# Output projection and second layer norm: two passes over halves of the token tiles become one pass over single tiles

## The chip, the cores and the metric

The kernel runs on the 8 cores of one Trainium2 chip. Each core computes one of the 8 sequences of the batch, with the same program and the same weights, and the cores exchange nothing. The time is the device time of the slowest core in microseconds (us).

## What is computed

One transformer layer with the norm behind each part, on x of shape (8, 2048, 2048): attention with its own norm ahead of it, 16 heads, a band of 256 tokens and 16 global tokens; then a gated feed-forward part whose weights are integers with a scale.

```python
xn = layernorm(x) * ln_scale + ln_bias
Q, K, V = proj(Wq), proj(Wk), proj(Wv)            # of [global tokens, xn]
attn = softmax(Q K^T * scale + band_mask)
a = (attn @ V)[:, 16:] @ Wo.T + x                 # the output projection
x = layernorm(x + a)                              # = layernorm(2 x + out @ Wo.T)
x = layernorm(x + ffn(x))                         # silu(gate) * up, then down
```

The change lies in the fourth and fifth of these lines: the output projection by Wo, the sum with 2x, and the norm of that sum.

## The kernel before

The kernel is written by hand: each engine has its own stream of instructions, in the order in which the program text emits them, and counts on semaphores are all that ties the streams together. `wt(engine, token)` makes an engine wait until a semaphore has reached a count. A wait holds up everything behind it in that engine's stream. SyncE (SP) issues most of the transfers, so a wait in its stream holds up every transfer that is written behind it. `barrier()` makes all engines wait for everything before it.

The stages follow one another: the first norm and its transposes; per head the projections and the attention (its result goes to `ao_dram` in HBM, line 641); a barrier (line 649); the stage that the change touches (lines 672 to 771); a barrier (line 773); then the feed-forward part in two passes over half of the tokens each. It first reads the normed tiles back from `r2_dram` (GpSimd, line 808), transposes them on TensorE (line 1124), and then runs gate, up and down.

The stage of the change, before it: the 2048 tokens are 16 tiles of 128 rows. Wo, in bf16, is held in SBUF as four slices of 512 output columns (`woT`), loaded by 16 transfers on GpSimd's queue that cast from f32 (line 677). Two halves `th` of 8 token tiles follow each other. Within a half:

- For each half of the output columns `eh` and each of the 8 tiles `ti`, SP loads the attention result of that tile, 512 KB in bf16, into one of two buffers `aot` (line 697). TensorE makes two accumulation groups of 16 matmuls of 128x512 (line 713), one per slice of Wo, into two PSUM banks in turn, and VectorE copies each bank into the tile's slot of `v1h` (line 726). `v1h` holds 8 tiles in f32. So every attention tile is loaded twice, and the half has 32 groups.
- After that, a loop over the 8 tiles does the norm. SP loads the tile of x (1 MB, line 739, two buffers `xres`); VectorE adds 2x (line 749), takes the statistics (lines 296 and 299), ScalarE the root (line 306), VectorE the reciprocal (line 313) and the normed tile (line 760); SP stores the tile to `r2_dram` (line 767), which waits for line 760.

In SP's stream the order of this second loop is therefore: x load of tile ti, store of tile ti (behind a wait for its norm), x load of tile ti+1, its store, and so on. Behind the last store of the first half come the attention loads of the second half. The wait of the load itself (line 738) asks only for the norm two tiles back.

VectorE's first copy of the second half also waits for all stores of the first half (`t_spill_half`, line 724), because it overwrites the slots of `v1h`.

Of the kernel before, what the change touches and what calls it, by code (L numbers as in the profile page):

```python
# [10 lines left out]
ALU = mybir.AluOpType  # L11
bfdt = ml_dtypes.bfloat16

D = 2048
T = 2048
NH = 16
# [6 lines left out]
ND = D // 128  # L23
# [26 lines left out]
def wt(eng, token):  # L50
    if token is None:
        return
    sem, n = token
    if n > 0:
        eng.wait_ge(sem.h, n)
# [10 lines left out]
def build_nc(debug=False):  # L66
    nc = bass.Bass("TRN2", target_bir_lowering=False)

    x_in = nc.dram_tensor("x", [T, D], F32, kind="ExternalInput").ap()
# [21 lines left out]
    r2_dram = nc.dram_tensor("r2sp", [T, D], F32, kind=scratch_kind).ap()  # L91
    ao_dram = nc.dram_tensor("aosp", [NT, NH, 128, 128], BF16, kind=scratch_kind).ap()
# [5 lines left out]
    s_pe = Sem(nc, "s_pe")  # L98
    s_dve = Sem(nc, "s_dve")
# [10 lines left out]
    s_aot = [Sem(nc, "s_aot0"), Sem(nc, "s_aot1")]  # L110
    s_xr = [Sem(nc, "s_xr0"), Sem(nc, "s_xr1")]
    s_r2s = Sem(nc, "s_r2s")
# [33 lines left out]
    agm = sba(outer, "agt", [128, 2], F32)  # L146
    rstd = sba(outer, "rstdt", [128, 1], F32)
# [18 lines left out]
    with nc.Block() as blk:  # L166
# [34 lines left out]
        def f(sync):  # L201
            for dst, src in [(ident, id_in), (masks, mk_in), (ones_col, oc_in),
                             (ones_row, or_in), (neg128, n128_in), (lnw, lnw_in),
                             (lnb, lnb_in), (sgt, sg_in), (sut, su_in),
                             (sd_row, sd_in)]:
                s_c0.inc(sync.dma_start(out=dst[:, :], in_=src[:, :]), 16)
# [82 lines left out]
        def emit_ln_stats(get_v, tok_ready):  # L289
            def f(dve):  # L290
                wt(dve, tok_ready)
                wt(dve, ln_act_tok["prev"])
                dve.wait_ge(s_dve.h, s_dve.n)
                vv = get_v()
                for i in range(4):
                    ins = dve.bn_stats(stats[:, i * 6:(i + 1) * 6], vv[:, i * 512:(i + 1) * 512])  # L296
                s_dve.inc(ins)
                dve.wait_ge(s_dve.h, s_dve.n)
                s_dve.inc(dve.bn_aggr(agm[:, :], stats[:, :]))
            blk.vector(f)  # L300
            t_ag = s_dve.tok

            def f(act, t_ag=t_ag, t_prev=ln_dve_tok["prev"]):
                wt(act, t_ag)
                wt(act, t_prev)
                return act.activation(sqv[:, :], agm[:, 1:2], AF.Sqrt, bias=epsv[:, 0:1])
            t_sq = da_emit(f)
            ln_act_tok["prev"] = t_sq

            def f(dve):  # L310
                wt(dve, t_sq)
                dve.wait_ge(s_dve.h, s_dve.n)
                s_dve.inc(dve.reciprocal(rstd[:, :], sqv[:, :]))
            blk.vector(f)
            ln_dve_tok["prev"] = s_dve.tok
            return s_dve.tok

        xt_tok = {}
        for tt in range(NT):
            buf = tt % 2  # L320
# [10 lines left out]
            t_rstd = emit_ln_stats(lambda buf=buf: xtile[:, buf * D:(buf + 1) * D], xt_tok[tt])  # L331
# [12 lines left out]
            for c in range(ND):  # L344
                bank = trb[(tt * ND + c) % 6]
# [83 lines left out]
        for hg in range(4):  # L429
# [7 lines left out]
            for h in range(4 * hg, 4 * hg + 4):  # L437
# [9 lines left out]
                for step in range(9):  # L447
                    bank = next_sc()
# [46 lines left out]
                if h % 4 == 0:  # L495
                    for kt in range(NT + 1):
                        bank = next_sc()
# [38 lines left out]
                for q4 in range(4):  # L536
                    klist = kts(q4) + ["glob"]
                    nk = len(klist)
                    for i, kt in enumerate(klist):
                        bank = next_sc()  # L540
# [115 lines left out]
        v1h = sba(p3s, "v1ht", [128, 8 * D], F32)  # L656
        woT = sba(p3s, "woTt", [128, 2 * ND * 1024], BF16)
# [22 lines left out]
        blk.gpsimd(f)  # L680
        t_wosl = [s_wos[sl].tok for sl in range(4)]

        for th in range(2):
            for eh in range(2):

                for ti in range(8):
                    tt = th * 8 + ti
                    abuf = ti % 2

                    def f(sync, th=th, eh=eh, ti=ti, tt=tt, abuf=abuf):  # L690
                        prev = t_womm.get((th, eh, ti - 2)) or t_womm.get((th, eh - 1, 6 + ti)) \
                            or t_womm.get((th - 1, 1, 6 + ti))
                        wt(sync, prev)
                        src_ = ao_dram[tt].rearrange("h p k -> p h k")
                        dstv = aot[:, abuf * D:(abuf + 1) * D].rearrange(
                            "p (h k) -> p h k", h=NH)
                        s_aot[abuf].inc(sync.dma_start(out=dstv, in_=src_), 16)
                    blk.sync(f)
                    t_aotld[(th, eh, ti)] = s_aot[abuf].tok

                    for e2 in range(2):
                        e4 = 2 * eh + e2
                        bank = b_wo[e2]

                        def f(t, th=th, eh=eh, ti=ti, e2=e2, e4=e4, abuf=abuf, bank=bank):
                            if th == 0 and ti == 0:
                                wt(t, t_wosl[e4])
                            if e2 == 0:
                                wt(t, t_aotld[(th, eh, ti)])
                            wt(t, bank.freed)  # L710
                            off = eh * ND * 1024 + e2 * ND * 512
                            for hc in range(NH):
                                ins = t.matmul(bank.p[:, :],  # L713
                                               aot[:, abuf * D + hc * 128:abuf * D + (hc + 1) * 128],
                                               woT[:, off + hc * 512:off + (hc + 1) * 512],
                                               start=(hc == 0), stop=(hc == NH - 1))
                            bank.used = s_pe.inc(ins)
                            t_womm[(th, eh, ti)] = bank.used
                        blk.tensor(f)

                        def f(dve, th=th, eh=eh, ti=ti, e2=e2, e4=e4, bank=bank):
                            wt(dve, bank.used)
                            if eh == 0 and e2 == 0 and th >= 1:
                                wt(dve, t_spill_half.get(th - 1))
                            dve.wait_ge(s_dve.h, s_dve.n)
                            ins = dve.tensor_copy(v1h[:, ti * D + e4 * 512:ti * D + (e4 + 1) * 512],
                                                  bank.p[:, :])
                            bank.freed = s_dve.inc(ins)
                        blk.vector(f)
                        t_woev[(th, eh, ti, e2)] = s_dve.tok  # L730
                t_womm[(th, eh)] = s_pe.tok

            for ti in range(8):
                tt = th * 8 + ti
                buf = ti % 2

                def f(sync, th=th, ti=ti, tt=tt, buf=buf):
                    wt(sync, t_ln2.get((th, ti - 2)) or t_ln2.get((th - 1, 6 + ti)))
                    s_xr[buf].inc(sync.dma_start(out=xres[:, buf * D:(buf + 1) * D],
                                                 in_=x_in[tt * 128:(tt + 1) * 128, :]), 16)  # L740
                blk.sync(f)
                t_xres[(th, ti)] = s_xr[buf].tok

                def f(dve, th=th, ti=ti, buf=buf):
                    wt(dve, t_xres[(th, ti)])
                    wt(dve, t_woev[(th, 1, ti, 1)])
                    vv = v1h[:, ti * D:(ti + 1) * D]
                    dve.wait_ge(s_dve.h, s_dve.n)
                    s_dve.inc(dve.scalar_tensor_tensor(vv, xres[:, buf * D:(buf + 1) * D],
                                                       2.0, vv, ALU.mult, ALU.add))  # L750
                blk.vector(f)
                t_v1 = s_dve.tok

                t_rstd = emit_ln_stats(lambda ti=ti: v1h[:, ti * D:(ti + 1) * D], t_v1)

                def f(dve, th=th, ti=ti, t_rstd=t_rstd):
                    wt(dve, t_rstd)
                    vv = v1h[:, ti * D:(ti + 1) * D]
                    dve.wait_ge(s_dve.h, s_dve.n)
                    s_dve.inc(dve.tensor_scalar(vv, vv, agm[:, 0:1], rstd[:, 0:1],  # L760
                                                ALU.subtract, ALU.mult))
                blk.vector(f)
                t_ln2[(th, ti)] = s_dve.tok

                def f(sync, tt=tt, ti=ti, t_r2=s_dve.tok):
                    wt(sync, t_r2)
                    s_r2s.inc(sync.dma_start(out=r2_dram[tt * 128:(tt + 1) * 128, :],
                                              in_=v1h[:, ti * D:(ti + 1) * D]), 16)
                blk.sync(f)
                t_spill[(th, ti)] = s_r2s.tok  # L770
            t_spill_half[th] = s_r2s.tok

        barrier()
        p3p.close()
# [520 lines left out]
```

## Time and profile before

| | us |
|---|---|
| time before, median of 2 runs | 5431.15 |
| these 2 runs | 5306.09 and 5556.21 |
| the profiled execution, device time | 5057.47 |
| its span on the slowest core (core 2) | 5055.9 |
| spans of the 8 cores | 5029.0 to 5055.9 |
| mean granted TensorE clock of the cores | 0.909 to 0.913 |

The span runs from the first to the last instruction of a core, so 1.6 us of the profiled execution lie outside it. The profiled execution is 5% shorter than the lower one of the two timed runs, so a duration of the trace can be set against 5057.47 us only. TensorE is busy for 75% of the span, VectorE for 27%, ScalarE for 8%. The stage of the change lies between 1651 and 2176 us of the span, a tenth of it. All positions in the text are microseconds from the span's start on core 2.

### The profile page before, as it was taken

The page shows a single profiled execution, that of the slowest core. Times are in us where ns is not written, and L with a number is a line of the kernel's source. Part 1 is how long each engine was busy: PE and PEld are TensorE (multiplying, and loading weights), DVE is VectorE, ACT ScalarE, POOL GpSimd, SP SyncE. Part 2 cuts the span into 40 slices and gives each one's busy share as a digit, 9 for nine tenths or more (in the row PEclk, how much of TensorE's full clock was granted, in tenths as well). Part 3 has the DMA queues.
Part 4 walks back from the last instruction along what each step waited for, and adds up shares of the span by engine and source line. Part 5 has one row for each costly group of instructions (what it writes and reads, how often), then busy time and mean ns, then how long its engine had stood idle before and what let it go on. Part 6 is the DMA issues. An engine that isn't in the chain of part 4 may idle for free.

```text
span 5055.9 us, 44219 instructions; the slowest of 8 cores (5029.0 to 5055.9 us)
## 1 busy us (share of the span) xinstructions
PE 3768.4 (75%) x15764; PEld 1444.9 (29%) x16072; DVE 1343.3 (27%) x1936; ACT 402.7 (8%) x661; POOL 315.4 (6%) x601
## 2 busy tenths in 40 slices
PE   2288898988988536269999986556799999766640
PEld 1133232333332212123333332222233333222210
DVE  6624534444354132331111110000222221000013
ACT  0001212111122000000000000000011110000000
POOL 0000000000000000000000011111000000111110
PEclk9999898999998777669999999989999999999985
DMA  2211202102000533343333334333444443244344
GB/s 83 65 28 20 38 13 41 23 15 40 13 17 17 109 116 93 124 84 67 67 60 66 67 65 73 52 57 59 90 114 110 115 100 65 28 60 60 58 90 158
DMA packets 236584, 331.02 MB, mean 65 GB/s; under 512 B 133316, under 2 KB 178373, under 8 KB 225621
## 3 DMA queue, kind: packets, MB, share of 16 engines
q0 software_dynamic: 85856, 180.46, 22.3%
q1 hardware_dynamic: 150518, 147.72, 9.1%
q8 instruction: 136, 2.23, 0.2%
q14 instruction: 74, 0.61, 0.0%
HBM read 445.62 MB, written 58.72 MB: 100 GB/s over the span
## 4 chain that ended last, share of the span: by engine, by line
PE 65%; DMA 16%; DVE 10%; issue 6%; ACT 1%; SPq 1%; DVEq 0%; another core or an unknown queue 0%; POOL 0%; ACTq 0%; POOLq 0%
PE p_gu L913 25%; DMA wdTt<-wd 10%; PE p_wo L713 4%; PE p_sc L458 4%; PE p_sc L470 4%; PE p_sc L506 4%; PE p_gu L1023 3%; PE p_gu L916 2%; PE p_srow L1221 2%; DVE statst L296 2%; PE p_pv L1219 2%; DMA xrest<-x 2%; PE p_sc L552 2%; DVE xnfmt L362 2%; PE p_s L1023 2%
## 5 line engine op out<-in xcount | busy, mean ns | idle before, releaser
L913 PE MATMUL p_gu<-xn2ht,wgTt 128*128 128x512 bf16 x2740 | 633.1, 381 | 15.4 <-DVE rowLt L875 9.0
L913 PE MATMUL p_gu<-xn2ht,wuTt 128*128 128x512 bf16 x2766 | 635.8, 380 | 2.6
L944 DVE TENSOR_SCALAR gust<-p_gu,sutt 128x512 f32<-128x512 f32 x176 | 132.2, 751 | 1102.6 <-PE p_gu L918 1101.4
L1023 PE MATMUL p_cs<-wdTt,hmidt 128*128 128x512 bf16 x336 | 132.7, 395 | 375.5 <-DMA wdTt<-wd 300.6
L1023 PE MATMUL p_gu<-wdTt,hmidt 128*128 128x512 bf16 x1378 | 377.9, 396 | 39.9 <-DVE v2spt L1050 16.5
L913 PEld LDWEIGHTS p_gu<-xn2ht,wgTt 128*128 128x128 bf16 x2816 | 262.1, 98 | 376.5 <-issue 87.8
L913 PEld LDWEIGHTS p_gu<-xn2ht,wuTt 128*128 128x128 bf16 x2816 | 261.1, 98 | 365.6 <-issue 74.7
L713 PE MATMUL p_wo<-woTt,aott 128*128 128x512 bf16 x1004 | 230.6, 391 | 176.9 <-DMA aott<-aosp 142.9
L571 ACT ACTIVATE p_sbt<-p_sc 128x512 bf16<-128x512 f32 x352 | 203.2, 596 | 1027.6 <-PE p_sc L555 1010.2
L1050 DVE TENSOR_TENSOR v2spt<-p_cs,sd_bct 128x512 f32<-128x512 f32 x8 | 5.5, 692 | 1012.5 <-PE p_cs L1032 1012.5
L934 ACT ACTIVATE gust<-p_gu,sgtt 128x512 f32<-128x512 f32 x176 | 120.9, 687 | 1843.9 <-PE p_gu L918 1830.3
L1009 POOL DMA_DIRECT2D wdTt<-wd x352 | 185.8, 528 | 1036.3 <-PE p_x L1023 922.2
L458 PE MATMUL p_sc<-xnfmt,wqkTt 128*128 128x512 bf16 x1003 | 223.9, 381 | 27.3 <-DMA wqkTt<-wk 26.2
L1219 PE MATMUL p_pv<-p_sbt,v4t 128*128 128x512 bf16 x340 | 150.6, 443 | 105.0 <-DVE rowAt L587 83.2
L470 PE MATMUL p_sc<-xnfmt,wqkTt 128*128 128x512 bf16 x1004 | 221.9, 379 | 1.1
L506 PE MATMUL p_sc<-wvTt,xnfmt 128*128 128x512 bf16 x1003 | 220.4, 379 | 1.1
L1023 PE MATMUL p_s<-wdTt,hmidt 128*128 128x512 bf16 x690 | 216.1, 394 | 0.9 <-issue 0.2
L594 DVE RECIPROCAL rowBt<-rowAt 1x512 f32<-1x512 f32 x64 | 213.8, 3341 | 6.6
L1023 PEld LDWEIGHTS p_cs<-wdTt,hmidt 128*128 128x128 bf16 x352 | 34.9, 99 | 559.1 <-issue 558.5
L713 PEld LDWEIGHTS p_wo<-woTt,aott 128*128 128x128 bf16 x1024 | 102.3, 100 | 305.5 <-issue 191.5
L1023 PEld LDWEIGHTS p_gu<-wdTt,hmidt 128*128 128x128 bf16 x1408 | 140.8, 100 | 145.8 <-issue 28.5
L353 PE MATMUL p_tr<-identt,n1t 128*128 128x128 bf16 x256 | 56.9, 266 | 153.1 <-DVE n1t L337 125.7
(121 smaller groups left out, 3079.0 us busy)
## 6 DMA issues: line engine op xcount, KB each, us to landing
wgTt<-wg POOLq DMA_DIRECT2D x88, 512.0 KB, 5.1
wuTt<-wu POOLq DMA_DIRECT2D x88, 512.0 KB, 7.1
wdTt<-wd POOLq DMA_DIRECT2D x352, 128.0 KB, 2.9
xtilet<-x SPq DMA_DIRECT2D x16, 1024.0 KB, 5.8
aott<-aosp SPq DMA_DIRECT2D x32, 512.0 KB, 4.1
xrest<-x SPq DMA_DIRECT2D x16, 1024.0 KB, 6.9
r2sp<-v1ht SPq DMA_DIRECT2D x16, 1024.0 KB, 4.8
v2sp<-v2spt SPq DMA_DIRECT2D x64, 256.0 KB, 2.0
```

Source lines behind the costliest of these rows:

```text
L458: ins = t.matmul(bank.p[:, :], wqkT[:, dc * 128:(dc + 1) * 128], xnfm[:, dc * T + q4 * 512:dc * T + (q4 + 1) * 512], start=(dc == 0), stop ...
L470: ins = t.matmul(bank.p[:, :], wqkT[:, D + dc * 128:D + (dc + 1) * 128], xnfm[:, dc * T + q4 * 512:dc * T + (q4 + 1) * 512], start=(dc == ...
L506: ins = t.matmul(bank.p[:, :], xnfm[:, dc * T + kt * 128:dc * T + (kt + 1) * 128], wvT[:, dc * 512:(dc + 1) * 512], start=(dc == 0), stop= ...
L571: return act.activation(p_sb[:, (i % 4) * 512:(i % 4 + 1) * 512], bank.p[:, :], AF.Exp)
L594: s_dve.inc(dve.reciprocal(rowB[:, sl], rowA[:, sl]))
L713: ins = t.matmul(bank.p[:, :], aot[:, abuf * D + hc * 128:abuf * D + (hc + 1) * 128], woT[:, off + hc * 512:off + (hc + 1) * 512], start=( ...
L913: t.matmul(bank.p[:, :], wsl[:, j * D + dc * 128:j * D + (dc + 1) * 128], xn2h[:, dc * 1024 + tc * 512:dc * 1024 + (tc + 1) * 512], start= ...
L934: return act.activation(gus[:, 0:512], bg.p[:, :], AF.Silu, scale=sgt[:, hb:hb + 1])
L944: ins = dve.tensor_scalar(gus[:, 512:1024], bu.p[:, :], sut[:, hb:hb + 1], None, ALU.mult)
L1009: s_wd[j].inc(pool.dma_start(out=wdT[:, j * 512:(j + 1) * 512], in_=wd_in[e4, hb * 128:(hb + 1) * 128, :]), 16)
L1023: ins = t.matmul(pd_banks[ti].p[:, :], hmid[:, hb * 1024 + ti * 128:hb * 1024 + (ti + 1) * 128], wdT[:, j * 512:(j + 1) * 512], start=(hb ...
L1219: t.matmul(bpv.p[:, :], v4[:, kt * 512 + hh * 128:kt * 512 + (hh + 1) * 128], p_sb[:, (i % 4) * 512:(i % 4 + 1) * 512], start=first, stop= ...
```

## The change

The loops over token halves and over halves of the output columns go. One loop over the 16 tiles `tt` does, for each tile: one attention load, the four groups of 16 matmuls (one per slice of Wo, into the two banks in turn) with their four copies, then the x load, the sum, the statistics, the norm and the store. Each attention tile is loaded once. The slots of `v1h` are reused after 8 tiles, and the first copy of a tile from the ninth on waits for the store of the tile just before. On every engine the work of the tile's norm now stands ahead of the next tile's work.

The core of the diff (in the new loop, the bodies of the functions that stay are left out):

```diff
@@ -680,95 +680,84 @@
-        for th in range(2):
-            for eh in range(2):
-
-                for ti in range(8):
-                    tt = th * 8 + ti
-                    abuf = ti % 2
...
-            for ti in range(8):
-                tt = th * 8 + ti
-                buf = ti % 2
...
+        for tt in range(16):
+            ti = tt % 8
+            abuf = tt % 2
+            buf = tt % 2
+
+            def f(sync, tt=tt, abuf=abuf):
+                wt(sync, t_womm.get(tt - 2))
+                src_ = ao_dram[tt].rearrange("h p k -> p h k")
...
+                s_aot[abuf].inc(sync.dma_start(out=dstv, in_=src_), 16)
+            blk.sync(f)
+            t_aotld[tt] = s_aot[abuf].tok
+
+            for e4 in range(4):
+                bank = b_wo[e4 % 2]
+
+                def f(t, tt=tt, e4=e4, abuf=abuf, bank=bank):
+                    if tt == 0:
+                        wt(t, t_wosl[e4])
+                    if e4 == 0:
+                        wt(t, t_aotld[tt])
+                    wt(t, bank.freed)
+                    off = e4 * ND * 512
+                    for hc in range(NH):
...
+                def f(dve, tt=tt, ti=ti, e4=e4, bank=bank):
+                    wt(dve, bank.used)
+                    if tt >= 8 and e4 == 0:
+                        wt(dve, t_spill.get(tt - 1))
                     dve.wait_ge(s_dve.h, s_dve.n)
...
+            t_womm[tt] = s_pe.tok
+
+            def f(sync, tt=tt, buf=buf):
+                wt(sync, t_ln2.get(tt - 2))
+                s_xr[buf].inc(sync.dma_start(out=xres[:, buf * D:(buf + 1) * D],
+                                             in_=x_in[tt * 128:(tt + 1) * 128, :]), 16)
+            blk.sync(f)
...
+            t_rstd = emit_ln_stats(lambda ti=ti: v1h[:, ti * D:(ti + 1) * D], t_v1)
...
+            def f(sync, tt=tt, ti=ti, t_r2=s_dve.tok):
+                wt(sync, t_r2)
+                s_r2s.inc(sync.dma_start(out=r2_dram[tt * 128:(tt + 1) * 128, :],
+                                          in_=v1h[:, ti * D:(ti + 1) * D]), 16)
+            blk.sync(f)
+            t_spill[tt] = s_r2s.tok
```

## Rows read from the trace of the kernel before

**Rows 1.** Waits, 1640 to 2240: engine line waited for: us in total, times, longest.

```profile
POOL n2pt L808 <- issue: 515.7, 1, 515.7
PE p_wo L713 <- DMA aott<-aosp: 142.9, 2, 125.0
DVE v1ht L749 <- DMA xrest<-x: 106.3, 14, 7.7
PE p_wo L713 <- DMA woTt<-wo: 32.7, 2, 24.5
```

**Rows 2.** Windows, core 2: stretch, length, busy by engine (instructions), granted clock, DMA share, GB/s.

```profile
1720.00:1815.00 95.00, 94.53 (x433) 43.08 (x440) 19.36 (x28) 0.00 (x0) 0.00 (x0) 1.00 0.35 84
1815.00:1940.00 125.00, 1.72 (x8) 0.59 (x6) 53.00 (x65) 3.64 (x9) 0.00 (x0) 0.52 0.38 130
1940.00:2058.00 118.00, 112.97 (x502) 50.74 (x512) 23.98 (x33) 0.00 (x0) 0.00 (x0) 0.97 0.34 77
2058.00:2176.00 118.00, 0.00 (x0) 0.00 (x0) 50.46 (x64) 2.36 (x8) 0.00 (x0) 0.51 0.37 133
```

**Rows 3.** Timeline, one tile of the norm to the next: start, us, instruction.

```profile
1842.05 0.32 SPq L767 DMA_DIRECT2D r2sp<-v1ht  x1
1842.46 0.39 SPq L739 DMA_DIRECT2D xrest<-x  x1
1849.62 2.29 DVE L749 SCALAR_TENSOR_TENSOR v1ht<-xrest,v1ht 128x2048 f32<-128x2048 f32 x1 [7.64 <-DMA xrest<-x]
```

**Rows 4.** Timeline, from the first half's last norm into the second half.

```profile
1932.41 1.35 DVE L760 TENSOR_SCALAR v1ht<-v1ht,agt,rstdt 128x2048 f32<-128x2048 f32 x1 [0.18 <-DVE rstdt L313]
1933.83 0.32 SPq L767 DMA_DIRECT2D r2sp<-v1ht  x1
1934.24 107.56 SPq L697 DMA_DIRECT2D aott<-aosp  x16
...
1941.68 113.49 PE L713 MATMUL p_wo<-woTt,aott 128*128 128x512 bf16 x502 [124.97 <-DMA aott<-aosp]
...
1948.37 0.69 DVE L726 COPY v1ht<-p_wo 128x512 f32<-128x512 f32 x1 [14.62 <-PE p_wo L713]
...
1958.66 0.69 DVE L726 COPY v1ht<-p_wo 128x512 f32<-128x512 f32 x1 [2.69 <-PE p_wo L713]
```

**Rows 5.** Timeline, the last copy, its norm, and the stage's last norm.

```profile
2055.35 0.69 DVE L726 COPY v1ht<-p_wo 128x512 f32<-128x512 f32 x1 [2.76 <-PE p_wo L713]
2056.15 2.29 DVE L749 SCALAR_TENSOR_TENSOR v1ht<-xrest,v1ht 128x2048 f32<-128x2048 f32 x1
...
2062.47 1.35 DVE L760 TENSOR_SCALAR v1ht<-v1ht,agt,rstdt 128x2048 f32<-128x2048 f32 x1 [0.18 <-DVE rstdt L313]
...
2169.33 1.35 DVE L760 TENSOR_SCALAR v1ht<-v1ht,agt,rstdt 128x2048 f32<-128x2048 f32 x1 [0.18 <-DVE rstdt L313]
```

**Rows 6.** Loads of Wo: first and last issue, us from issue to landing.

```profile
L677 POOL DMA_DIRECT2D woTt<-wo x16: 528/596/662, 1652.1 to 1659.9; - x16
DMA to landing us min/median/max: 10.4/31.7/52.2
```

**Rows 7.** Timeline, start of the stage: a restart of TensorE and its copy.

```profile
1710.67 4.42 PE L713 MATMUL p_wo<-woTt,aott 128*128 128x512 bf16 x10 [17.98 <-DMA aott<-aosp]
...
1716.74 0.69 DVE L726 COPY v1ht<-p_wo 128x512 f32<-128x512 f32 x1 [23.19 <-PE p_wo L713]
```

**Rows 8.** Chain of waits, the first norm of the stage: start, us, what.

```profile
1816.89 0.70 DVE v1ht L726
...
1825.30 1.36 DVE v1ht L760
```

**Rows 9.** Attention loads issued at 1934.2 and 1934.7: issue ns, and landing.

```profile
L697 SPq DMA_DIRECT2D aott<-aosp x2: 387/2200/4014, 1934.2 to 1934.7; - x2
DMA to landing us min/median/max: 7.2/8.0/8.7
```

**Rows 10.** The load issued at 1803.0, an x load behind it: landing.

```profile
L697 SPq DMA_DIRECT2D aott<-aosp x1: 360/360/360, 1803.0 to 1803.0; - x1
DMA to landing us min/median/max: 4.1/4.1/4.1
```

More of the change, by code:

```diff
@@ L681, in build_nc @@
         t_wosl = [s_wos[sl].tok for sl in range(4)]
-        for th in range(2):
-            for eh in range(2):
-                for ti in range(8):
-                    tt = th * 8 + ti
-                    abuf = ti % 2
[L690 to L731, printed above, removed]
-            for ti in range(8):
-                tt = th * 8 + ti
-                buf = ti % 2
[L737 to L747, printed above, removed]
@@ new lines, in build_nc @@
+        for tt in range(16):
[5 more added lines that the diff above has]
+                src_ = ao_dram[tt].rearrange("h p k -> p h k")
+                dstv = aot[:, abuf * D:(abuf + 1) * D].rearrange(
+                    "p (h k) -> p h k", h=NH)
+                s_aot[abuf].inc(sync.dma_start(out=dstv, in_=src_), 16)
[11 more added lines that the diff above has]
+                    for hc in range(NH):
+                        ins = t.matmul(bank.p[:, :],
+                                       aot[:, abuf * D + hc * 128:abuf * D + (hc + 1) * 128],
+                                       woT[:, off + hc * 512:off + (hc + 1) * 512],
+                                       start=(hc == 0), stop=(hc == NH - 1))
+                    bank.used = s_pe.inc(ins)
+                blk.tensor(f)
+                def f(dve, tt=tt, ti=ti, e4=e4, bank=bank):
+                    wt(dve, bank.used)
+                    if tt >= 8 and e4 == 0:
+                        wt(dve, t_spill.get(tt - 1))
@@ L748, in f @@
                     dve.wait_ge(s_dve.h, s_dve.n)
-                    s_dve.inc(dve.scalar_tensor_tensor(vv, xres[:, buf * D:(buf + 1) * D],
-                                                       2.0, vv, ALU.mult, ALU.add))
+                    ins = dve.tensor_copy(v1h[:, ti * D + e4 * 512:ti * D + (e4 + 1) * 512],
+                                          bank.p[:, :])
+                    bank.freed = s_dve.inc(ins)
                 blk.vector(f)
-                t_v1 = s_dve.tok
-                t_rstd = emit_ln_stats(lambda ti=ti: v1h[:, ti * D:(ti + 1) * D], t_v1)
@@ L756, in f @@
[L756 to L768, printed above, removed]
@@ L769, in build_nc @@
-                blk.sync(f)
-                t_spill[(th, ti)] = s_r2s.tok
-            t_spill_half[th] = s_r2s.tok
+                t_woev[(tt, e4)] = s_dve.tok
+            t_womm[tt] = s_pe.tok
[4 more added lines that the diff above has]
+            blk.sync(f)
+            t_xres[tt] = s_xr[buf].tok
@@ new lines, in f @@
+            def f(dve, tt=tt, ti=ti, buf=buf):
+                wt(dve, t_xres[tt])
+                wt(dve, t_woev[(tt, 3)])
+                vv = v1h[:, ti * D:(ti + 1) * D]
+                dve.wait_ge(s_dve.h, s_dve.n)
+                s_dve.inc(dve.scalar_tensor_tensor(vv, xres[:, buf * D:(buf + 1) * D],
+                                                   2.0, vv, ALU.mult, ALU.add))
+            blk.vector(f)
+            t_v1 = s_dve.tok
+            t_rstd = emit_ln_stats(lambda ti=ti: v1h[:, ti * D:(ti + 1) * D], t_v1)
@@ new lines, in f @@
+            def f(dve, ti=ti, t_rstd=t_rstd):
+                wt(dve, t_rstd)
+                vv = v1h[:, ti * D:(ti + 1) * D]
+                dve.wait_ge(s_dve.h, s_dve.n)
+                s_dve.inc(dve.tensor_scalar(vv, vv, agm[:, 0:1], rstd[:, 0:1],
+                                            ALU.subtract, ALU.mult))
+            blk.vector(f)
+            t_ln2[tt] = s_dve.tok
+            def f(sync, tt=tt, ti=ti, t_r2=s_dve.tok):
+                wt(sync, t_r2)
+                s_r2s.inc(sync.dma_start(out=r2_dram[tt * 128:(tt + 1) * 128, :],
+                                          in_=v1h[:, ti * D:(ti + 1) * D]), 16)
```

## The prediction

> **What bounds the kernel now.** I read the page first, for the share of each engine, and then only the stage that the diff rewrites. TensorE's 75% says little about that stage, so I cut it into windows [rows 2]. The reader is to see two kinds of stretch in turn. In the two stretches of matmuls TensorE is busy for nearly all of the time (94.53 of 95 us, 112.97 of 118 us) at a granted clock of about 1.0, its upper level of 2.4 GHz. In the two stretches of norms TensorE does next to nothing, the clock is at 0.5 (1.2 GHz), and VectorE is busy for only 53.00 of 125 us and 50.46 of 118 us. So while the norms run, no engine is full.
>
> The waits say what the norms wait for: VectorE waits 106.3 us in 14 portions of up to 7.7 us for the load of x [rows 1]. The timeline says why that load is late. It is issued at 1842.46, 0.41 us after the store of the tile before [rows 3]. By its own wait it could have been issued a tile earlier: it asks only for the norm two tiles back. It is late because the store ahead of it in SP's stream waits for a norm. This order is the most important fact for the change.
>
> The same order makes TensorE's longest wait. It stands 125.0 us for an attention tile [rows 1]. The buffer of that tile has been free since the last matmul of the first half, around 1816, but its load is issued at 1934.24, right behind the store of the half's last norm [rows 4]. In this kernel an attention load that is written behind a norm's store starts only after the norm.
>
> **What the change removes.** Half of the attention loads, 16 of 32. They cost nothing on the path: a load in a matmul stretch lands in 4.1 us [rows 10], two groups of matmuls take about 6.9 us (a third of the 10.29 us between the first and the fourth copy [rows 4] is 3.43 a group), there are two buffers, and TensorE is full there [rows 2]. Their removal is worth 0. If the cover were gone each would cost at most its 4.1 us. The number of matmuls (64 groups of 16), of copies (64), of norms (16), of x loads and of stores stays.
>
> **What it puts in another order.** SP's stream is now, for each tile: attention load, x load, store (behind a wait for this tile's norm), attention load of the next tile. So each attention load has a norm's store ahead of it, where before one in 32 had (the one at 1934.24). TensorE waits for this load, the copies wait for TensorE, the norm waits for the fourth copy, and the store waits for the norm. All of it is one chain; the second buffers don't help, since what would fill them is never issued early.
>
> One turn of this chain, for the tiles 1 to 15, with each link from the one place in the trace where it occurs:
>
> - from the end of the norm of the tile before (1932.41 + 1.35 = 1933.76) over store issue, load issue and landing to the first matmul (1941.68): 7.92 us [rows 4];
> - from the first matmul to the first copy, with the clock starting low: 6.69 us (1941.68 to 1948.37) after a long pause [rows 4] and 6.07 us (1710.67 to 1716.74) after a pause of 17.98 us [rows 7]. I take the middle, 6.38;
> - from the first to the fourth copy: 1958.66 - 1948.37 = 10.29 us [rows 4];
> - from the fourth copy over its 0.69 us to the sum: 2056.15 - 2055.35 = 0.80 us [rows 5];
> - from the sum to the end of the norm: 2062.47 + 1.35 - 2056.15 = 7.67 us [rows 5].
>
> That is 7.92 + 6.38 + 10.29 + 0.80 + 7.67 = 33.06 us, and 15 x 33.06 = 495.9 us. With 6.07 or 6.69 in the second link it is 32.75 or 33.37, so 491.2 or 500.5 us.
>
> The clock: TensorE stands for 7.92 + 0.69 + 0.11 + 7.67 = 16.4 us in each turn. After the pause of 17.98 us the first 10 matmuls took 4.42 us, 0.44 each, against 3.43 / 16 = 0.214 later in a group; so the clock had fallen in a pause of about this length [rows 7]. Hence I charge each tile a slow start. The 17 us burst that follows is long enough to be fast again, since the fourth copy came 10.29 us after the first even after the long pause.
>
> The x load is issued right behind the attention load, 0.4 us or so later. The same sequence of store and x load takes 7.16 us from issue to use [rows 3]; with an attention load between, add at most its 4.1. That is 11.3 us, and the sum comes 6.38 + 10.29 + 0.80 = 17.5 us after the first matmul. So the x loads, which set the pace of the norms before, are now covered, and cost 0. The wait for the store of the tile before at each first copy (from the ninth tile on) costs 0 too: the copy comes 7.92 + 6.38 = 14.3 us after the norm, while the store is issued 0.07 us after it and everything it and two attention loads needed had landed by 1934.7 + 8.7 = 1943.4, 9.6 us after the norm [rows 9]. On VectorE the next tile's copies stand behind the norm, but they are not there to be done before it.
>
> The first tile: all four slices of Wo are needed for it, where the old order needed two. The last of the 16 loads is issued at 1659.9 and, if it has the longest landing, is in at 1659.9 + 52.2 = 1712.1 [rows 6]. The old order was stopped just as long, by the second attention tile, until 1710.67 [rows 7]. From 1712.1 the fourth group needs 6.38 us to its copy, and the first norm, which is longer than the later ones, ends 1825.30 + 1.36 - 1816.89 = 9.77 us after the copy's start [rows 8]: 1728.2.
>
> **The sum.** The last norm ends at 1728.2 + 495.9 = 2224.1, against 2169.33 + 1.35 = 2170.7 before [rows 5]: 53.4 us later, with the bounds of the slow start 48.4 to 58.4. What follows (store, barrier, GpSimd's read back, which has waited for this all along [rows 1], transposes) is unchanged and moves with it. Put another way: before, the norms ran at the pace of their loads, 15.3 us each ((2169.33 - 2062.47) / 7 [rows 5]), and the matmuls ran on their own; now a turn of 33.1 us stands for 4 groups (13.7 us when fast) and a norm (15.3), so it costs 4 us more than the sum of both.
>
> Against the profiled execution: 5057.47 + 53.4 = 5110.9 us. The two timed runs lie 249 and 499 us above it, with nothing in the trace to say where. I add the difference to the median shown: 5431.15 + 53.4 = 5484.6 us, 1.0% more. For the range the executions of the same kernel count for more than my terms: from 5057.47 + 48 = 5105 to 5556.21 + 59 = 5615.
>
> **Two rules beside it.** The trace has the attention load landing in 4.1 us by itself [rows 10] and in 7.2 us behind a store [rows 9], and the sum goes by the second. The Trainium skill, "DMA: Bandwidth & Descriptors", section "Anatomy of one DMA", gives for a transfer on GpSimd's path 2.0 us plus the bytes at 436 GB/s; for 512 KB that is an estimate of 3.2 us, and with it a turn would be 4.0 us shorter, and the whole 7 us faster than before instead of 53 slower. The trace doesn't agree, for this load with its short pieces on SP's queue, so the measurement decides. The same page, section "Queues, rings and completion order", says that each DMA engine takes the descriptors of one queue in ring order. By that rule an x load can't delay the attention load ahead of it, which would leave the 53 and rule out the second rival below; the trace agrees at the one place it has, the load at 1803.0 [rows 10].
>
> **The rivals.**
>
> 1. *Norms and matmuls overlap, faster.* This is what the order of the loops suggests: while VectorE norms a tile, TensorE does the next. It needs the next attention load to be issued before the norm ends. Then from 1718.5 on (copy of the first tile's fourth group) 15 tiles of 4 x 3.43 = 13.7 us follow, 206 us, and one norm with its copy's 0.80, 8.5 us: the end at 1933, 238 us earlier, 5193 us. For it speaks that VectorE's own work, 53 us for 8 tiles' norms or 6.6 us a tile and 4 x 0.69 of copies, fits under 13.7 us. Against it speak rows 3 and 4, both places where a load stands behind a norm's store. It would also need only the load to be early, nothing else. Chance 0.05.
>
> 2. *The x load disturbs the attention load, slower by over 2%.* In the trace the attention load behind a store landed in 7.2 us with another attention load of 512 KB behind it, which landed 1.9 us later (1934.7 + 8.7 against 1934.2 + 7.2) [rows 9]. Now 1 MB stands behind it. If transfers shared the engines evenly, the attention tile would be in only when all three are. By the step of 1.9 us for 512 KB the larger transfer adds at least 3.8 us, and at most the 7.16 us that an x load takes to its use [rows 3]; with the middle, 5.5 us a turn, it is 82 us in all and 135 with the 53: 5567 us. It decides from (109 - 53) / 15 = 3.7 us a turn on, 109 us being 2%. Against it: the load at 1803.0 with an x load right behind it landed in 4.1 us [rows 10]. Chance 0.10.
>
> 3. *The clock stays low.* If the bursts never got the upper level, a tile would take 64 x 0.44 = 28.3 us to its last matmul and not 16.7: 11.6 us more, 174 us in all, with the 53 a loss of 227: 5658 us. Against it stands that each restart in the trace was fast within its first group. Chance 0.03.
>
> 4. *The turn is shorter than I say.* If the store ahead didn't delay the load, it would land in 4.1 and not 7.2 us: 3.1 us less a turn, 47 in all. If instead the clock didn't fall, the first group would take 3.43 + 0.3 or so and not 6.38: 2.6 less, 40 in all. Either leaves a loss of 6 to 14 us, 5437 to 5445 us, no measurable change. Chance 0.10.
>
> **How the numbers follow.** The forecast, one serial chain of about 33 us a tile, has 0.68; the rivals have 0.05, 0.10, 0.03 and 0.10, and 0.04 is left for what I haven't thought of. About 2% is what a measurement of this kernel can tell from no change. The forecast's 1.0% lies within that, but the runs of the kernel before spread by 4.7%, so I give a fifth of it to a measured loss of over 2% and a little to a gain: slower 0.10 + 0.03 + 0.12 = 0.25, faster 0.05 + 0.02 = 0.07, within 2% the rest, 0.68. The forecast's own range is +48 to +59 us. The range of the absolute time, 5105 to 5615, also takes in rivals 1, 2 and 4.
>
> **What would show it.** In the profile after: 16 attention loads, each issued about 0.5 us behind a store of the normed tile; TensorE waiting for `aott` about 15 times and some 16 us each, 240 us in all, with nothing of the 125 us wait left; VectorE's wait for x gone from 106 us to near nothing; the copies' start of one tile to the next 33 us apart; a granted clock of about 0.7 over the stage instead of stretches at 0.5 and 1.0; the last norm ending near 2224. Wrong it would be if attention loads were issued ahead of the store before them (rival 1), if their landing took 10 us or more (rival 2), or if the first copy came less than 5 us after the first matmul (rival 4).

## The result, and the profile after

| | us |
|---|---|
| changed kernel, median of 26 runs | 5311.0 (5107.01 to 5620.99) |
| kernel before, median of 25 runs | 5266.93 (5062.63 to 5556.21) |
| ratio | 1.0074, 95% interval 1.0048 to 1.0100 |
| profiled execution of the changed kernel, device time | 5112.67 |
| its span on the slowest core (core 4) | 5111.1 |
| spans of its 8 cores | 5080.6 to 5111.1 |

The changed kernel is slower by 0.74%: beyond the uncertainty of the measurement, and within 2%. In many executions of either kernel the cores of one die, or of both, show a lower granted clock; that is why the medians lie some 200 us above the profiled executions, and the ratio leaves those executions out.

The predicted chain is there, tile after tile. The timeline of the changed kernel shows one whole turn (start, us, instruction; L757 is the store, L693 the attention load, L729 the x load, L708 the matmuls, L720 the copy, L739 the sum, L750 the norm):

```profile
1826.14 0.32 SPq L757 DMA_DIRECT2D r2sp<-v1ht  x1
1826.55 0.39 SPq L693 DMA_DIRECT2D aott<-aosp  x1
1827.03 4.12 SPq L729 DMA_DIRECT2D xrest<-x  x1
1833.91 16.50 PE L708 MATMUL p_wo<-woTt,aott 128*128 128x512 bf16 x63 [16.55 <-DMA aott<-aosp]
1840.22 0.69 DVE L720 COPY v1ht<-p_wo 128x512 f32<-128x512 f32 x1 [14.16 <-PE p_wo L708]
...
1850.59 0.69 DVE L720 COPY v1ht<-p_wo 128x512 f32<-128x512 f32 x1 [2.76 <-PE p_wo L708]
1851.45 2.29 DVE L739 SCALAR_TENSOR_TENSOR v1ht<-xrest,v1ht 128x2048 f32<-128x2048 f32 x1 [0.17 <-DVE v1ht L720]
...
1857.77 1.35 DVE L750 TENSOR_SCALAR v1ht<-v1ht,agt,rstdt 128x2048 f32<-128x2048 f32 x1 [0.18 <-DVE rstdt L313]
1859.19 0.32 SPq L757 DMA_DIRECT2D r2sp<-v1ht  x1
1859.60 0.39 SPq L693 DMA_DIRECT2D aott<-aosp  x1
...
1866.95 15.35 PE L708 MATMUL p_wo<-woTt,aott 128*128 128x512 bf16 x63 [16.54 <-DMA aott<-aosp]
```

Everything waits in a ring: load for store, matmuls for load, copy for matmuls, norm for copy, store for norm. TensorE stands for 16.5 to 17.9 us ahead of each of the 15 tiles. The waits of the stage, 1640 to 2300, answer to rows 1:

```profile
PE p_wo L708 <- DMA aott<-aosp: 250.6, 15, 17.8
PE p_wo L708 <- DMA woTt<-wo: 44.9, 4, 27.7
DVE v1ht L739 <- DVE v1ht L720: 2.8, 16, 0.2
```

Before, TensorE had two waits for an attention tile, 142.9 us in all [rows 1]; now it has 15, 250.6 us in all. VectorE's wait for x (106.3 us [rows 1]) is gone: the sum now follows the copy by 0.2 us. What the x loads no longer cost comes back in TensorE's waits. The windows of before and after over the stage show the same work in more time (length, busy by engine, granted clock, DMA share, GB/s). Of the kernel before:

```profile
1651.00:2171.00 520.00, 230.57 (x1004) 102.32 (x1024) 148.88 (x192) 6.00 (x17) 8.44 (x16) 0.72 0.42 111
```

Of the changed kernel:

```profile
1651.00:2218.00 567.00, 263.22 (x1004) 108.60 (x1024) 148.84 (x192) 5.99 (x17) 8.45 (x16) 0.71 0.33 88
```

VectorE is busy for the same 149 us. TensorE has the same 1004 recorded matmuls and is busy 32.7 us longer, since each tile's start is slow: in the turn shown the granted clock is 0.59 from the first matmul to the first copy, and 1.00 from there to the fourth copy. The rest is waiting. The two windows:

```profile
1833.90:1840.20 6.30, 6.29 (x18) 2.41 (x19) 0.00 (x0) 0.00 (x0) 0.00 (x0) 0.59 0.20 85
1840.20:1850.50 10.30, 10.16 (x47) 4.41 (x46) 2.08 (x3) 0.00 (x0) 0.00 (x0) 1.00 0.00 0
```

The stage starts at 1651.6 before and 1652.4 after (first attention load), and its last norm ends at 2170.7 [rows 5] and, with the last store at 2217.63, at 2217.6. So it takes 519.1 and 565.2 us: 46.1 us more. These are core 2 before and core 4 after, the slowest of each execution. Core by core, from the first attention load to the last store, the stage is 38.4 to 49.2 us longer.

The landing of the loads (all 16 attention loads, then all 16 x loads):

```profile
L693 SPq DMA_DIRECT2D aott<-aosp x16: 359/387/427, 1652.4 to 2185.0; - x16
DMA to landing us min/median/max: 7.0/7.1/8.7
L729 SPq DMA_DIRECT2D xrest<-x x16: 3773/4105/4175, 1652.8 to 2185.5; - x16
DMA to landing us min/median/max: 9.0/9.1/17.2
```

### The profile page after: what moved, and what is told of

It reads as the page before. It is cut to its first block, busy times and chain, and to the rows that moved or that the text cites. A ratio compares the mean times of both kernels' runs of the same rounds, so it can differ in the third digit from the quotient of the medians.

```text
span 5111.1 us, 44171 instructions; the slowest of 8 cores (5080.6 to 5111.1 us)
## 1 busy us (share of the span) xinstructions
PE 3811.6 (75%) x15764; PEld 1452.9 (28%) x16072; DVE 1342.6 (26%) x1936; ACT 402.9 (8%) x661; POOL 315.8 (6%) x601
## 4 chain that ended last, share of the span: by engine, by line
PE 65%; DMA 16%; DVE 10%; issue 6%; ACT 1%; SPq 1%; DVEq 0%; POOL 0%; ACTq 0%; another core or an unknown queue 0%; POOLq 0%
PE p_gu L902 24%; DMA wdTt<-wd 10%; PE p_wo L708 5%; PE p_sc L458 4%; PE p_sc L470 4%; PE p_sc L506 4%; PE p_gu L1012 3%; PE p_gu L905 2%; PE p_srow L1210 2%; DMA aott<-aosp 2%; DVE statst L296 2%; PE p_pv L1208 2%; PE p_sc L552 2%; DVE xnfmt L362 2%; PE p_s L1012 2%
## 5 line engine op out<-in xcount | busy, mean ns | idle before, releaser
L708 PE MATMUL p_wo<-woTt,aott 128*128 128x512 bf16 x1004 | 263.2, 427 | 297.1 <-DMA aott<-aosp 250.6
L708 PEld LDWEIGHTS p_wo<-woTt,aott 128*128 128x128 bf16 x1024 | 108.6, 107 | 452.2 <-issue 359.5
```

Source lines behind the costliest of these rows:

```text
L708: ins = t.matmul(bank.p[:, :], aot[:, abuf * D + hc * 128:abuf * D + (hc + 1) * 128], woT[:, off + hc * 512:off + (hc + 1) * 512], start=( ...
```

## The experiments

The theory: the wait for the norm, which stands ahead of the store in SP's stream, holds back the next attention load and makes the turn. The rivals: the transfers or the engines set the turn, whatever the order; the x load behind disturbs the attention load; the clock accounts for the loss; the dropped reloads were worth something. Each ratio below is to the kernel before, from the same chip.

### The store on another queue

```diff
             def f(sync, tt=tt, ti=ti, t_r2=s_dve.tok):
                 wt(sync, t_r2)
                 s_r2s.inc(sync.dma_start(out=r2_dram[tt * 128:(tt + 1) * 128, :],
                                           in_=v1h[:, ti * D:(ti + 1) * D]), 16)
-            blk.sync(f)
+            blk.gpsimd(f)
```

> The changed kernel with one difference: the store of the normed tile is issued by GpSimd and no longer by SP. Theory (the wait in SP's stream ties the tiles into one chain): attention and x loads are now issued early, so TensorE does two groups of the next tile during a norm, until its two banks are full. Without waiting for a load, a turn is 0.7 us, two more groups, a copy and the norm, 16 us, in the first half; in the second the first copy also waits for the store of the tile before (lands 5.2 us after its issue), 21.5 us. The last norm ends near 2013 instead of 2218, 205 us earlier (170 to 205 with slow starts of the clock): ratio to before 0.967 to 0.974. Rival (the transfers or the engines themselves set the 32.7 us): turn about 33 us as in the changed kernel, ratio 1.007.

Measured: 0.9792 (0.9766 to 0.9818). The wait has gone from SP's stream, and one word takes the changed kernel from 0.7% slower to 2.1% faster. The chain is shown. The gain is smaller than expected (0.967 to 0.974), and the stores tell where it stays. Two in the first half and two in the second half of the tiles (VectorE's copies behind them):

```profile
1784.60 0.53 POOL L757 DMA_DIRECT2D r2sp<-v1ht  x1 [16.19 <-DVE v1ht L750]
1801.32 0.53 POOL L757 DMA_DIRECT2D r2sp<-v1ht  x1 [16.19 <-DVE v1ht L750]
...
1907.86 0.53 POOL L757 DMA_DIRECT2D r2sp<-v1ht  x1 [26.83 <-DVE v1ht L750]
1935.19 0.53 POOL L757 DMA_DIRECT2D r2sp<-v1ht  x1 [26.80 <-DVE v1ht L750]
```

```profile
1916.60 1.49 DVE L720 COPY v1ht<-p_wo 128x512 f32<-128x512 f32 x2 [9.28 <-DMA r2sp<-v1ht]
```

The turn is 16.7 us in most of the first half (17.5 on average), near the 16 of the theory, and 27.3 in the second, where 21.5 were expected. The new wait for the store of the tile before, which cost nothing inside the serial chain, is now on the path, and at 9.3 us it is longer than the 5.2 us that I had taken from stores issued by SP. The bursts behind it also start slowly again (15.4 us for 64 matmuls, behind pauses of 11.9 us).

GpSimd's queue is not the reason for the long landing. SP now issues an x load of 1 MB 0.2 to 0.5 us ahead of each of the first 14 stores, and these land in 8.3 to 10.1 us. The last two stores have no x load ahead of them and land in 4.2 and 4.6 us. One of either kind:

```profile
L757 POOL DMA_DIRECT2D r2sp<-v1ht x1: 531/531/531, 1907.9 to 1907.9; - x1
DMA to landing us min/median/max: 8.6/8.6/8.6
L757 POOL DMA_DIRECT2D r2sp<-v1ht x1: 533/533/533, 2044.5 to 2044.5; - x1
DMA to landing us min/median/max: 4.2/4.2/4.2
```

### The attention load ahead of the store

```diff
+            if tt + 1 < 16:
+                load_a(tt + 1)
+
             def f(sync, tt=tt, ti=ti, t_r2=s_dve.tok):
                 wt(sync, t_r2)
```

(`load_a` is the load as it was, waiting for the matmuls of the tile that has its buffer; the first tile's load stands ahead of the loop. The x load stays behind the store.)

> The changed kernel with one difference: the attention load of the next tile is written ahead of this tile's store in SP's stream; the x load stays behind the store. Theory: TensorE's wait goes. The x load, issued 0.5 us behind a norm and landing 7 to 9 us later, is now just in time or up to 2 us late for the sum: turn 16 to 18 us in the first half and 21.5 us in the second, the whole 170 to 205 us shorter than the changed kernel, ratio 0.967 to 0.974, as with the store on GpSimd. Rival (x load sets the pace once the attention load is early, as it did before): turn of the norms 18 us or more everywhere and a wait for x of over 2 us each.

Measured: the profiled span is 4924.8 us, the fastest run 4926.34 against 5059.36 of before, 0.974; the four runs give no interval. The last store is issued at 2044.15, 173 us before that of the changed kernel: 18.0 us a turn in the first half, and 23.8 in the second, where 21.5 were expected. The load alone, a few lines higher in the same stream, does what the other queue did. The rival had x as the new pace; VectorE waits for it 0.8 us in all:

```profile
DVE v1ht L725 <- DMA r2sp<-v1ht: 43.3, 8, 5.5
PE p_wo L713 <- DMA aott<-aosp: 11.7, 6, 3.1
DVE v1ht L744 <- DMA xrest<-x: 0.8, 1, 0.8
```

### The same, with each copy waiting for its own slot's store

```diff
-                        wt(dve, t_spill.get(tt - 1))
+                        wt(dve, t_spill.get(tt - 8))
```

(with one semaphore for each of the 8 slots, so that the count is exact)

> The kernel with the attention load ahead of the store and two banks, with one more difference: the first copy of a tile waits for the store of its own slot, 8 tiles back, and not for that of the tile before. Theory: the wait of 5.4 us in each of the last 8 tiles goes, and with it the pause that lets the clock fall; the turn is 17 to 18 us throughout instead of 23.8 in the second half, the last norm about 50 us earlier than with the attention load ahead alone, ratio to before 0.963. Rival (the x load, issued behind the norm, is late for the shorter turn): turn 19 us or more.

Measured: 0.9632 (0.9604 to 0.9660). From the first store at 1730.81 to the last at 1993.63 it is 17.5 us a turn. From first to last store that is 262.8 us, where it was 316.4 with the wait for the tile before (1727.74 to 2044.15): once it was on the path, that wait was worth 54 us, or 1%.

### Both loads ahead, four banks

```diff
-                bank = b_wo[e4 % 2]
+                bank = b_wo[e4]
...
+            if tt + 1 < 16:
+                load_a(tt + 1)
+                load_x(tt + 1)
+
             def f(sync, tt=tt, ti=ti, t_r2=s_dve.tok):
```

(four PSUM banks in `b_wo`, and the slots' own stores as above)

> The changed kernel with both loads of the next tile written ahead of the store, four PSUM banks instead of two, and each slot's first copy waiting only for the store of its own slot (8 tiles back). Theory: TensorE alone sets the pace, 64 matmuls in 13.8 us a tile; the last norm ends at 1717.4 + 15 x 13.8 + 8.5 = 1933, 285 us before that of the changed kernel; ratio to before 0.953, granted clock about 1.0 in the stage. Rival (1 + 1 + 0.5 MB a tile is more than the transfers can do in 13.8 us, 181 GB/s): a turn of 15 to 18 us with waits for loads, ratio 0.957 to 0.968.

Measured: 0.9604 (0.9563 to 0.9646). That is the ratio of the rival and not the 0.953 of the theory, and TensorE still waits a little for most attention tiles:

```profile
1897.85 13.97 PE L725 MATMUL p_wo<-woTt,aott 128*128 128x512 bf16 x63 [1.19 <-DMA aott<-aosp]
1913.19 13.97 PE L725 MATMUL p_wo<-woTt,aott 128*128 128x512 bf16 x62 [1.37 <-DMA aott<-aosp]
```

The turn is 15.3 us there, and 15.6 on average ((1967.3 - 1733.4) / 15). Either the transfers had too little bandwidth, as the rival says, or the load was still issued too late, since it stands behind the store of the tile two before its own. The next kernel tells these apart. Four banks and the early x load came together here, so what each is worth alone stays open.

### The attention load two tiles ahead

```diff
+            if tt + 2 < 16:
+                load_a(tt + 2)
             if tt + 1 < 16:
-                load_a(tt + 1)
                 load_x(tt + 1)
```

> The kernel with four banks and loads ahead of the store, with the attention load now two tiles ahead instead of one (it waits only for the matmuls of the tile that has its buffer). In the kernel with one ahead TensorE still waited 1.2 to 1.9 us a tile for it. Theory: these waits go, turn 14.0 us instead of 15.4, the last norm 15 to 20 us earlier, ratio to before 0.956. Rival (2.5 MB in 14 us is too much for the transfers, 179 GB/s): the wait moves to x, turn stays at 15 us or more, ratio 0.960.

Measured: 0.9528 (0.9506 to 0.9550), the fastest kernel of this study, faster than theory (0.956) and rival (0.960) had it. So it was the order. Windows on core 0, and its matmuls:

```profile
1740.00:1920.00 180.00, 180.00 (x836) 81.61 (x834) 121.42 (x158) 3.83 (x13) 0.00 (x0) 1.00 0.58 194
```

```profile
1717.22 212.34 PE L726 MATMUL p_wo<-woTt,aott 128*128 128x512 bf16 x976 [5.91 <-DMA woTt<-wo]
```

TensorE is busy for 180 of 180 us at a granted clock of 1.00, all but the first three groups in one piece, with 194 GB/s of transfers beside it. The rival took 179 GB/s for too much; it falls.

### The kernel before with its store on GpSimd's queue

```diff
                     s_r2s.inc(sync.dma_start(out=r2_dram[tt * 128:(tt + 1) * 128, :],
                                               in_=v1h[:, ti * D:(ti + 1) * D]), 16)
-                blk.sync(f)
+                blk.gpsimd(f)
```

> The kernel before with one difference: the store of the normed tile is issued by GpSimd and no longer by SP. Theory (SP's order set the pace of the old norms as well): the 14 waits for x, 7.6 us each, go, and the wait of 125 us before the second half gets shorter with them; the norms run at VectorE's 8 to 9 us each; 105 to 115 us less, ratio 0.977 to 0.979. Rival (old norms limited by the transfers themselves, 134 GB/s): pace stays near 15 us, ratio 1.00.

Measured: 0.9767 (0.9744 to 0.9791). The old norms were held by the same wait, not by the transfers. The sums of the first half were 15.3 us apart on core 2. On core 7 of this run they are 7.8 to 9.1 us apart; three of them:

```profile
1851.87 2.29 DVE L749 SCALAR_TENSOR_TENSOR v1ht<-xrest,v1ht 128x2048 f32<-128x2048 f32 x1
1859.65 2.29 DVE L749 SCALAR_TENSOR_TENSOR v1ht<-xrest,v1ht 128x2048 f32<-128x2048 f32 x1
1867.42 2.29 DVE L749 SCALAR_TENSOR_TENSOR v1ht<-xrest,v1ht 128x2048 f32<-128x2048 f32 x1
```

With the store out of the way, the old order (0.9767) and the new one (0.9792) can't be told apart, since their intervals overlap: the new order has nothing to show for itself until its loads run ahead and its own wait for the store is cut.

### One load per tile, norms apart

The loops `for tt in range(8 * th, 8 * th + 8)` over loads and groups, and then over norms, for each half `th`; all else as in the changed kernel.

> One part of the change alone: one attention load and four groups per tile as in the changed kernel, but the norms in a loop of their own behind each 8 tiles, as before. Theory (the 16 loads that go were covered): last norm at the same place as in the kernel before, within 3 us; ratio 1.000. Rival (the reloads took something from TensorE or the transfers): up to 16 x 0.7 us less, ratio 0.998 or lower.

Measured: 1.0004 (0.9984 to 1.0023). From the first attention load at 1650.55 to the last norm's end at 2165.9 it is 515.4 us on core 1, 3.7 less than on core 2 before: a little more than the 3 us that I allowed, but from the first attention load to the last store the eight cores of the kernel before differ by more (512 to 523 us), and the runs show nothing of it. The 16 loads that the change saves are worth 0; all of the 0.74% comes from the place of the norms.

### What the store ahead costs the load

```diff
+            if tt + 1 < 16:
+                load_a(tt + 1, after=t_ln2[tt])
+
             def f(sync, tt=tt, ti=ti, t_r2=s_dve.tok):
                 wt(sync, t_r2)
```

(`after`: SP waits for this tile's norm ahead of the load too, so the chain stays serial)

> The changed kernel with one difference: SP issues the next attention load right after the norm's end and ahead of that tile's store, still behind the same wait for the norm. It measures what the store ahead costs the load. Theory (landing 7.1 us behind a store, 4.1 without): load issued 0.4 us earlier and landed 3.0 us sooner, turn 29.3 instead of 32.7 us, last norm 51 us earlier than in the changed kernel, ratio to before 0.997. Rival (a load with short pieces takes 7 us wherever nothing but a pause lies before it): turn 32.3, ratio 1.006.

Measured: 1.0002 (0.9976 to 1.0028), just above the 0.997 expected and below the 1.0074 of the changed kernel. Landing of the 16 attention loads:

```profile
L692 SPq DMA_DIRECT2D aott<-aosp x16: 359/371/371, 1649.4 to 2139.6; - x16
DMA to landing us min/median/max: 3.9/4.2/8.7
```

4.2 us where it was 7.1. The turn is 29.6 us (1725.00 to 2139.6, 14 turns), and the last norm comes 46.6 us earlier counted from the stage's start. So 3 us of each turn are the store's share of the transfer.

### What the clock's fall costs

```diff
+            def f(t):
+                for k in range(60):
+                    t.matmul(p_fill[:, :], woT[:, 0:128], woT[:, 0:512],
+                             start=True, stop=True)
+            if tt < 15:
+                blk.tensor(f)
```

> The changed kernel with 60 additional matmuls of 128x512 per tile, on Wo's own slice, into a PSUM bank that nobody reads, issued behind the tile's four groups; about 12.9 us, so they lie in TensorE's wait of 16.5 us. It measures what the clock's fall costs. Theory: the clock stays at its upper level, the tile's 64 matmuls take 14.0 us instead of 16.0 us on average, turn 30.6, last norm 31 us earlier, ratio to before 1.001. Rival (the slow start is not the clock but the load or the weights): burst still 16 us, ratio 1.007.

Measured: 1.0077 (1.0057 to 1.0096), the rival's number. But the bursts show that this was not its reason: they were of both kinds behind pauses of the same length.

```profile
1804.14 15.46 PE L709 MATMUL p_wo<-woTt,aott 128*128 128x512 bf16 x63 [3.57 <-DMA aott<-aosp]
...
1836.12 13.97 PE L709 MATMUL p_wo<-woTt,aott 128*128 128x512 bf16 x63 [3.58 <-DMA aott<-aosp]
...
1866.63 16.63 PE L709 MATMUL p_wo<-woTt,aott 128*128 128x512 bf16 x63 [3.59 <-DMA aott<-aosp]
```

The turn had become 32.0 us. So this kernel doesn't decide it. The next is the same with `range(72)`:

> As the kernel with 60 additional matmuls, but with 72 of them, 15.5 of the 16.5 us of TensorE's wait. With 60, pauses of 3.6 to 4.9 us were left, and of the 15 bursts behind them some took 14.0 us and others up to 16.7; the granted clock was still at its lower level at 1771 to 1777. Theory (the clock's fall in the pause is all of the slow start): with 1 us of pause every burst takes 14.0 us, turn 30.6 us, last norm about 31 us earlier than in the changed kernel, ratio to before 1.001. Rival (something else in the restart): bursts of 15 us and more stay.

Measured: 1.0040 (1.0020 to 1.0060), where 1.001 was expected, just below the interval. On core 2, 14 of 15 bursts take 13.97 us, and the windows give the clock at 1.00 throughout:

```profile
1797.26 13.97 PE L709 MATMUL p_wo<-woTt,aott 128*128 128x512 bf16 x63 [1.23 <-DMA aott<-aosp]
1827.82 13.97 PE L709 MATMUL p_wo<-woTt,aott 128*128 128x512 bf16 x63 [1.05 <-DMA aott<-aosp]
```

```profile
1740.00:2180.00 440.00, 420.63 (x1910) 189.49 (x1946) 131.77 (x172) 4.12 (x14) 0.00 (x0) 1.00 0.26 84
```

The turn there is 30.8 us against 32.7, so the clock's fall costs the changed kernel 1.9 us a tile, 28 us in all, by the traces; that is 0.55%. The ratios of the two kernels, 1.0040 and 1.0074, lie 0.34% apart with intervals that overlap: the runs don't contradict the traces, and don't settle the size either. The Trainium skill, "TensorE: Matmul & The Clock Gate", section "HAM oscillation", describes this pattern, a burst of matmuls behind a wait for a transfer that starts at the lower clock every time; the trace of the changed kernel agrees, with 15 bursts of 15 to 17 us for what takes 14.0.

The changed kernel was run once more, on the chip of the kernels with the norms apart, with the load ahead of the store and with 60 matmuls more. Its 8 runs give no interval. Their lowest is 5102.87 us, against 5046.05 for the kernel before: 1.011, just above what was expected. On that chip the lowest run with the load ahead of the store is 5046.46, and with 60 matmuls more 5085.01, so both lie below the changed kernel there too.

> The changed kernel as it is, for the three others on the same chip. Turn 32.7 us, ratio 1.005 to 1.010.

## Why the prediction was right or wrong

The mechanism and the sign were right, and the difference was a little too large; the base that it was added to was wrong. I forecast 5484.6 us and 5311.0 were measured.

- **The step that failed is the base.** I added the difference to the median of the two runs shown, 5431.15 us. Over 25 runs the median of the same kernel is 5266.93, 164 us lower. Two runs 250 us apart, with the profiled execution 249 us below the lower, carried no median. Taken against 5266.93 my number reads as a loss of 4.1%, four times what I meant; 5266.93 + 53.4 would have been 5320.3. The range held the time only because I had widened it by that spread. The sum on the profiled execution, 5110.9 us, is what the trace supported: the profiled execution after took 5112.67 us, and the lowest of the 26 runs is 5107.01. That it fits to 2 us is in part luck. Of the 55.2 us between the two profiled executions 46.1 lie in the stage, 0.8 ahead of it and 8.3 behind it, where nothing was changed.
- **The difference.** 53.4 us by the sum; 46.1 in the stage by the two traces; 0.74% of 5062.63 us (the lowest run before), 37 us (24 to 51), by the runs. The forecast's own range of 48 to 59 lies above the trace's value. I had also written that 2% is about what a measurement can tell from no change; the interval here is 0.5% wide, and 0.74% is a measured loss.
- **The turn.** 33.06 us forecast, 32.69 measured ((2217.63 - 1727.31) / 15), 5.6 us over 15 tiles. Load issue and landing: 7.92 forecast, 7.84 in the turn shown (1826.07 to 1833.91). From the fourth copy to the sum: 0.80 forecast, 0.86. The norm 7.67 and 7.67. The term of the difference that was mis-sized is the slow start: 6.38 us to the first copy, from the middle of two rows; measured in the two turns around 1833.91 and 1866.95 it is 6.31 and 5.17, over all 15 5.94 on average. 15 x 0.44 = 6.6 us.
- **The first tile.** Forecast 76.6 us from the first load (1651.6) to its norm's end (1728.2), measured 74.8 (1652.4 to 1727.2). These 1.8 and the 5.6 make up the 7.3 between 53.4 and 46.1.
- **The reloads worth 0**: right, 1.0004 with this part alone. **The x loads covered**: right, they left the list of waits. **The wait for the store before at no cost**: right in the changed kernel, where it is hidden in the chain; it costs 5.4 to 9.3 us a tile as soon as the chain is cut.
- **Rival 1** (overlap): it didn't happen, for the reason given. Its price was right and its condition was not: I wrote that it needs only the load to be early, nothing else. The load ahead of the store alone gained 133 us of its 238 (4926.34 against 5059.36). All of it, 0.9528 or 239 us, came only with the copies' wait for their own slot, four banks and the load two tiles ahead.
- **Rival 2** (x load disturbs): out. The attention load lands in 7.1 us with 1 MB behind it, 7.2 before with 0.5 MB [rows 9].
- **Rival 3** (clock stays low): out, each burst was fast after its first group. **Rival 4**: both of its parts exist, 3.1 us for the store ahead and 1.9 for the clock, but the changed kernel pays them both, as forecast.

## What to carry to other kernels

- In a stream that is executed in order, look at what stands behind each wait. A store that waits for the end of a tile's work, written ahead of the next tile's load, turns a double-buffered loop into a serial chain; moving the load ahead of the store took this stage from 32.7 us a tile to 18.0 in the first half and 23.8 in the second, waiting for the own slot's store to 17.5 throughout, and four banks and the load two tiles ahead to 13.8.
- Fusing two loops pays only when the engines that shared the work can overlap. Check the issuing queue, the accumulators and the slots for it, one after the other: here each was the next limit (load behind the store, store wait of the wrong tile, two banks, one tile ahead).
- Take the forecast's base from the same execution as its terms, and treat a median of two distant runs as no base.

## What was not expected of the hardware

- A store of 1 MB on GpSimd's queue landed in 4.2 and 4.6 us by itself, and in 8.3 to 10.1 us with an x load of 1 MB issued on SP's queue 0.2 to 0.5 us ahead of it. From SP, ahead of the loads, it was 5.2 us in the median. So the other queue freed SP's stream here, and the transfers still slowed each other.
- A pause of TensorE of 3.6 us ended sometimes in a fast and sometimes in a slow start (13.97, 15.46, 16.63 us for the same burst), one of 16.5 us always in a slow one, the 14 of 0.7 to 1.7 us on core 2 with 72 matmuls more in none. There, pauses of 2.3 to 2.5 us ended in both (2.50 us on core 2 and 2.25 on core 1 slow, 2.33 and 2.27 on core 3 fast).
- The issue of an x load right behind an attention load held SP for 4.1 us, against 0.39 for one behind a store. It cost nothing here, since SP then waits anyway.
